# Attention in a fused two-layer block: scores from one 128-row product per head padded with zero rows, and row maxima from 48 rows in one half of the partitions, issued in twos behind two scores

## The reference, cut to what matters

```python
q = (x @ wq.T).reshape(B, S, 16, 8)          # B=4, S=1024, head size 8
k = repeat((x @ wk.T).reshape(B, S, 4, 8), 4) # four heads share one key/value head
v = repeat((x @ wv.T).reshape(B, S, 4, 8), 4)
attn = einsum('bqhd,bkhd->bhqk', q, k) / sqrt(8)
attn = softmax(where(causal, attn, -inf))
out = einsum('bhqk,bkhd->bqhd', attn, v).reshape(B, S, 128) @ wo.T
```

## Time and profile before

| | us |
|---|---|
| median of 3 runs | 1437.51 |
| lowest and highest | 1436.49, 1439.12 |
| profiled execution, span | 1437.3 |
| PE busy | 1150.2 (80%) |
| DVE busy | 1108.8 (77%) |
| ACT busy | 740.2 (51%) |
| POOL busy | 677.0 (47%) |

### The profile page before, as it was taken

The page is one execution under the profiler, slowest core; times in us unless marked ns, Lnnn a source line. Parts: engine busy times, 40 slices in busy tenths (PEclk is TensorE's granted clock), DMA queues, the critical chain, the costliest instruction groups (busy, mean ns, idle before and its releaser), DMA issues. The chain is left out here.

```text
span 1437.3 us, 18717 instructions
## 1 busy us (share of the span) xinstructions
PE 1150.2 (80%) x5568; PEld 535.7 (37%) x5568; DVE 1108.8 (77%) x3046; ACT 740.2 (51%) x1619; POOL 677.0 (47%) x823
## 2 busy tenths in 40 slices
PE   3613896899998997775747677998999899989885
PEld 1201454555554554331412322343334333433232
DVE  5889555655788879689897697788998889888227
ACT  4644676137435444342321157575567556755772
POOL 7524584364777778657670022215331533153312
PEclk9855997999999998787877589999999999999998
DMA  4000101422111110003123120303020302000002
GB/s 115 0 0 1 49 2 26 142 75 69 54 37 44 44 40 6 0 1 65 24 48 55 39 47 1 66 1 55 1 38 1 55 1 38 1 4 1 4 1 59
DMA packets 33682, 47.02 MB, mean 33 GB/s; under 512 B 5023, under 2 KB 18207, under 8 KB 33279
## 3 DMA queue, kind: packets, MB, share of 16 engines
q1 hardware_dynamic: 30990, 43.84, 13.8%
q10 hardware_dynamic: 2592, 2.00, 0.5%
HBM read 39.14 MB, written 6.68 MB: 32 GB/s over the span
## 5 line engine op out<-in xcount | busy, mean ns | idle before, releaser
L1694 ACT ACTIVATE RB<-PS 128x512 f32<-128x512 f32 (+3 forms) x768 | 323.2, 502 | 183.3 <-PE PS L676 180.4
L624 PE MATMUL PS<-B 96*128 96x512 bf16 (+3 forms) x768 | 247.6, 349 | 44.2 <-DVE SS L1191 14.7
L676 PE MATMUL PS<-B 96*128 96x512 bf16 (+3 forms) x768 | 238.3, 333 | 24.2 <-ACT RB L1694 22.2
L1191 DVE CUSTOM_DVE_ANT_0 PS<-PS,w_msk 128x128 f32<-128x128 f32 (+3 forms) x512 | 242.4, 505 | 18.6 <-PE PS L624 18.1
L1964 POOL TENSOR_SCALAR_AFFINE_SELECT RB<-RB 128x512 f32<-128x512 f32 x128 | 81.0, 635 | 363.9 <-ACT RB L1694 363.9
L1194 DVE TENSOR_REDUCE SS<-PS 128x1 f32<-128x512 f32 x256 | 175.6, 686 | 32.9 <-PE PS L624 31.9
L693 PE MATMUL PS<-RB,B 128*32 128x512 f32 (+3 forms) x1536 | 169.0, 514 | 0.0
L624 PEld LDWEIGHTS PS<-B 96*128 96x128 bf16 x768 | 75.0, 99 | 228.8 <-DVE SS L1191 99.7
L1870 POOL TENSOR_TENSOR RB<-RB,B 128x512 f32<-128x512 f32 x64 | 82.2, 1286 | 89.3 <-DVE RB L1020 66.8
L676 PEld LDWEIGHTS PS<-B 96*128 96x128 bf16 x768 | 73.6, 98 | 105.7 <-ACT RB L1694 74.6
L1536 ACT ACTIVATE RB<-PS 128x512 f32<-128x512 f32 x72 | 42.8, 595 | 129.6 <-PE PS L438 129.5
(11 more groups left out here) (262 smaller groups left out, 2209.9 us busy)
## 6 DMA issues: line engine op xcount, KB each, us to landing
B<-scrW SPq DMA_DIRECT2D x128, 128.0 KB, 3.0
B<-scrQ SPq DMA_DIRECT2D x72, 128.0 KB
scrQ<-B SPq DMA_DIRECT2D x6, 384.0 KB, 3.7
B<-scrK SPq DMA_DIRECT2D x36, 64.0 KB
X<-in_x SPq DMA_DIRECT2D x8, 256.0 KB, 8.7
out_dram<-X SPq DMA_DIRECT2D x7, 256.0 KB, 3.2
B<-in_w SPq DMA_DIRECT2D x3, 576.0 KB, 4.9
B<-in_zeros SPq DMA_DIRECT2D x9, 128.0 KB
```

Source lines behind the costliest of these rows:

```text
L624: pe.matmul(p[:, 0:w], qs[u % 3][:, h, 128 * i:128 * i + 128], keys_of(u, h)[:, 512 * c:512 * c + w], start=True, stop=True).then_inc(s["m ...
L676: pe.matmul(p[:, 0:w], keys_of(u, 4 * kl + z)[:, 128 * kt:128 * kt + 128], qs[u % 3][:, 4 * kl + z, 512 * qc + off:512 * qc + 512], start= ...
L1191: ins = dve.tensor_tensor_reduce(p, p, msk[:, 512 - w:512], 1.0, LOWEST, ALU.add, ALU.max, MX[:, u % 2, i, h, c:c + 1])
L1694: act.activation(RB[:, 4 * (step % 3) + z, 0:w], bank(bank_of["score", step, z])[:, 0:w], ACT.Exp).then_inc(s["ex2"], 1)
```

## The change

The rows of the contraction are laid out anew. `qs` and `kst` take all 128 partitions. For even heads (side 0) the nine product groups of 8 rows lie at rows 0 to 71, guard rows at 72 to 74, and zeros (ones in `kst`) down to 127. For odd heads (side 1) the first eight groups lie at rows 64 to 127, the ninth at 0 to 7, guard rows at 8 to 10, and zeros (ones) at 8 to 63. The six largest products come first, so they fill rows 0 to 47 for side 0 and 64 to 111 for side 1.

`score_2` contracts all 128 rows. `first_1` contracts only the 48 rows of the six largest products (the guard value that is subtracted from the scores leaves the three smallest out). Maxima are issued in twos, an odd head and an even head with the same tile, and on PE the order in a step becomes score, score, maximum, maximum, score, score, maximum, maximum. In steps 0 to 19 there are 4 or 6 maxima a step in place of 5.

So that heads of both key heads of a unit alternate, the columns of `wq` and the rows of `wo` are permuted on the host (`turn`). The `zrow` DMA falls away. `load_q` and `load_k` issue 18 DMAs of half the size; `fill_q` and `fill_k` issue 2 each, of 448 KB and 224 KB; the way home of the guard is 2 DMAs.

```diff
-        qs = [B[i][0:96, 0:4096].bitcast(BF).rearrange("p (h t) -> p h t", h=8) for i in (5, 1, 3)]
-        kst = [B[2][0:96, 2048 * i:2048 * i + 2048].bitcast(BF).rearrange("p (k t) -> p k t", k=4) for i in range(2)]
+        qs = [B[i][:, 0:4096].bitcast(BF).rearrange("p (s t) -> p s t", s=8) for i in (5, 1, 3)]
+        kst = [B[2][:, 2048 * i:2048 * i + 2048].bitcast(BF).rearrange("p (k l t) -> p k l t", k=2, l=2)
+               for i in range(2)]
...
-        FIRST = [(h, i, c) for h in range(8) for i in range(8) for c in range(i // 4 + 1)]
+        FIRST = [(2 * pair + side, i, c) for pair in range(4) for i in range(8) for c in range(i // 4 + 1)
+                 for side in (1, 0)]
+        PRODUCTS = [(0, 0), (0, 1), (1, 0), (1, 1), (0, 2), (2, 0), (1, 2), (2, 1), (2, 2)]
+        HIGHEST_ROWS = 48
+        GUARD_ROW = (72, 8)
+        SPARE_ROWS = (slice(72, 128), slice(8, 64))
+
+        def product_row(side, r):
+            return (64 * side + 8 * r) % 128
...
             if step < 20:
-                return [(1, n) for n in range(5 * step, min(5 * step + 5, 96))]
+                done = sum(6 if q % 5 in (1, 3) else 4 for q in range(step))
+                return [(1, n) for n in range(done, done + (6 if step % 5 in (1, 3) else 4))]
...
         def keys_of(u, h):
-            return kst[u // 2 % 2][:, 2 * (u % 2) + h // 4, :]
+            return kst[u // 2 % 2][:, u % 2, h % 2, :]
+
+        def queries_of(u, h):
+            return qs[u % 3][:, h, :]
+
+        def highest_rows(h):
+            return slice(64 * (h % 2), 64 * (h % 2) + HIGHEST_ROWS)
...
-                pe.matmul(p[:, 0:w], qs[u % 3][:, h, 128 * i:128 * i + 128],
-                          keys_of(u, h)[:, 512 * c:512 * c + w], start=True, stop=True).then_inc(s["mm1"], 1)
+                pe.matmul(p[:, 0:w], queries_of(u, h)[highest_rows(h), 128 * i:128 * i + 128],
+                          keys_of(u, h)[highest_rows(h), 512 * c:512 * c + w], start=True, stop=True).then_inc(s["mm1"], 1)
...
                 if u < 8 and r == 0:
-                    pe.wait_ge(s["gd1"], 16 * (u + 1))
-                for z in range(4):
-                    for v, n in ahead[z:z + 1]:
+                    pe.wait_ge(s["gd1"], 32 * (u + 1))
+                for half in range(2):
+                    for z in (2 * half, 2 * half + 1):
+                        if step < 192:
+                            score_2(step, z)
+                    for v, n in ahead[2 * half:2 * half + 2] if half == 0 else ahead[2:]:
                         first_1(next_1(step), v, n)
-                    if step < 192:
-                        score_2(step, z)
-                for v, n in ahead[4:]:
-                    first_1(next_1(step), v, n)
...
             def load_q(u):
                 b, hh = divmod(u, 2)
-                for a in range(3):
-                    for c in range(3):
-                        sp.dma_start(qs[u % 3][32 * a + 8 * c:32 * a + 8 * c + 8, :, :],
-                                     scrQ[b, a, 64 * hh:64 * hh + 64, :].rearrange("(h d) t -> d h t", d=8)).then_inc(
-                                         s_q[u % 3], 16)
-                if u >= 3:
-                    sp.dma_start(qs[u % 3][24:27, :, :], I["zrow"]).then_inc(s_q[u % 3], 16)
+                src = scrQ[b, :, 64 * hh:64 * hh + 64, :].rearrange("a (q l d) t -> a l d q t", q=4, l=2)
+                for r, (a, c) in enumerate(PRODUCTS):
+                    for side in range(2):
+                        o = product_row(side, r)
+                        sp.dma_start(qs[u % 3][o:o + 8, side:8:2, :], src[a, side, :, :, :]).then_inc(s_q[u % 3], 16)
...
-                sp.dma_start(qs[u % 3][24:27, :, :], scrM[u, :, :].rearrange("(a h) t -> a h t", h=8)).then_inc(s["gd1"], 16)
+                m3 = scrM[u, :, :].rearrange("(a q l) t -> l a q t", a=3, l=2)
+                for side in range(2):
+                    o = GUARD_ROW[side]
+                    sp.dma_start(qs[u % 3][o:o + 3, side:8:2, :], m3[side, :, :, :]).then_inc(s["gd1"], 16)
...
-    D["wqE"], D["wkE"], D["wvE"], D["woE"] = E("wq").T, E("wk").T, E("wv").T, E("wo").T
+    turn = np.arange(128).reshape(2, 2, 4, 8).transpose(0, 2, 1, 3).reshape(128)
+    D["wqE"], D["wkE"], D["wvE"], D["woE"] = E("wq").T[:, turn], E("wk").T, E("wv").T, E("wo").T[turn]
```

More of the change, by code:

```diff
@@ L629, in ready_1 @@
             def ready_1(u):
-                pe.wait_ge(s_q[u % 3], 192 + 160 * (u // 3))
-                pe.wait_ge(s_k[u // 2 % 2], 192 + 144 * (u // 4))
+                pe.wait_ge(s_q[u % 3], 32 + 288 * (u // 3 + 1))
+                pe.wait_ge(s_k[u // 2 % 2], 32 + 288 * (u // 4 + 1))
             value_c(0)
@@ L676, in score_2 @@
                 pe.matmul(p[:, 0:w], keys_of(u, 4 * kl + z)[:, 128 * kt:128 * kt + 128],
-                          qs[u % 3][:, 4 * kl + z, 512 * qc + off:512 * qc + 512],
+                          queries_of(u, 4 * kl + z)[:, 512 * qc + off:512 * qc + 512],
                           start=True, stop=True).then_inc(s["sc2"], 1)
@@ L692, in product_2 @@
                 for j in range(4):
-                    ins = pe.matmul(p[32 * j:32 * j + 32, off:off + w], VA[:, 8 * (u // 2) + kt, 2 * (u % 2) + kl, :],
+                    ins = pe.matmul(p[32 * j:32 * j + 32, off:off + w], VA[:, 8 * (u // 2) + kt, 2 * (u % 2) + j % 2, :],
                                     pb[:, j, 0:w], start=(kt == 0), stop=(kt == 4 * qc + 3), skip_group_check=True)
@@ L2008, in load_k @@
             def load_k(b):
-                for a in range(3):
-                    for c in range(3):
-                        sp.dma_start(kst[b % 2][32 * a + 8 * c:32 * a + 8 * c + 8, :, :],
-                                     scrK[c, :, 1024 * b:1024 * b + 1024].rearrange("(k d) t -> d k t", d=8)).then_inc(
-                                         s_k[b % 2], 16)
+                src = scrK[:, :, 1024 * b:1024 * b + 1024].rearrange("c (k l d) t -> c l d k t", k=2, l=2)
+                for r, (a, c) in enumerate(PRODUCTS):
+                    for side in range(2):
+                        o = product_row(side, r)
+                        sp.dma_start(kst[b % 2][o:o + 8, :, side, :], src[c, side, :, :, :]).then_inc(s_k[b % 2], 16)
             def load_q(u):
                 b, hh = divmod(u, 2)
-                for a in range(3):
-                    for c in range(3):
-                        sp.dma_start(qs[u % 3][32 * a + 8 * c:32 * a + 8 * c + 8, :, :],
-                                     scrQ[b, a, 64 * hh:64 * hh + 64, :].rearrange("(h d) t -> d h t", d=8)).then_inc(
-                                         s_q[u % 3], 16)
-                if u >= 3:
-                    sp.dma_start(qs[u % 3][24:27, :, :], I["zrow"]).then_inc(s_q[u % 3], 16)
+                src = scrQ[b, :, 64 * hh:64 * hh + 64, :].rearrange("a (q l d) t -> a l d q t", q=4, l=2)
+                for r, (a, c) in enumerate(PRODUCTS):
+                    for side in range(2):
+                        o = product_row(side, r)
+                        sp.dma_start(qs[u % 3][o:o + 8, side:8:2, :], src[a, side, :, :, :]).then_inc(s_q[u % 3], 16)
             def fill_q(u):
-                for a in range(3):
-                    sp.dma_start(qs[u][32 * a + 24:32 * a + 32, :, :], I["zeros"]).then_inc(s_q[u], 16)
+                for side in range(2):
+                    sp.dma_start(qs[u][SPARE_ROWS[side], side:8:2, :], I["zeros"]).then_inc(s_q[u], 16)
             def fill_k(b):
-                for a in range(3):
-                    sp.dma_start(kst[b][32 * a + 24:32 * a + 32, :, :], I["ones"]).then_inc(s_k[b], 16)
+                for side in range(2):
+                    sp.dma_start(kst[b][SPARE_ROWS[side], :, side, :], I["ones"]).then_inc(s_k[b], 16)
             def cuts_out(b):
@@ L2162, in arrays @@
     D["msk"] = np.concatenate([np.zeros((128, 384)), np.where(low, 0, -1e30)], axis=1).astype(bf)
-    D["zrow"] = np.zeros((3, 8, 1024), bf)
-    D["zeros"], D["ones"] = np.zeros((8, 8, 1024), bf), np.ones((8, 4, 1024), bf)
+    D["zeros"], D["ones"] = np.zeros((56, 4, 1024), bf), np.ones((56, 2, 1024), bf)
     return {k: np.ascontiguousarray(v) for k, v in D.items()}
```

## The result

The changed kernel takes **1483.4 us** (1479.7 to 1487.6) against 1437.2 for the kernel before on the same chip: a ratio of 1.0329, 95% interval 1.0301 to 1.0356, 46 us slower by the medians, 47 by the ratio. The prediction of 1442 us, with a range up to 1458, was wrong.

A forecast was written before the change was run, and what follows sets the result against it. PE and DVE were taken to pace the main stage in turn, PE's time counting in 63 of 164 steps. 1437.3 + 5 (rows, switches, overlap) + 0.3 (guard) = 1442.6, rounded down to 1442 us; range 1422 to 1458.

The forecast's parts named there:

- What bounds the kernel: Main stage, 820 to 1334 us: PE and DVE pace the loop in turn; ACT isn't the pace.
- the 63 waits of DVE: Main stage: DVE waits for a maximum's matmul, 45.2 us in all; PE time counts only in 63 of 164 steps.
- Overlap: A step's two pairs on PE: matmuls in opposite halves run side by side, saving 0.32 us a step.
- The stagger of the second start: Second matmul of a pair on PE: starts 0 to 0.05 us later; 0.03 us a step taken.
- Switches: PE's changes of array layout in a step: two round trips of 0.245 us less one 0.12 us switch, +0.37 us.
- The rival of cheap switches: Going to halves by rows costs as little as maximum to score: 1419 us, or 1430 at half price; chance 0.30.
- that of halves that don't overlap: Each maximum keeps its 0.163 us and layout changes come on top: 1461 us; chance 0.09.
- Net of the rows: PE in the main stage: -0.32 + 0.37 + 0.03 = +0.08 us a step, counted in 63 steps, +5 us.
- The order: PE's step, score, score, pair, score, score, pair, product: priced by added layout changes only, +0.37 us a step.
- the rival of a DVE that starves at the head of a step: First maximum behind two scores and a layout change, 0.53 us later: 33 us at worst, 1470; chance 0.07.
- Loads, guard, the stretch before 820: Twice the DMAs on SP and 740 to 820 us: nothing; the guard's way home, exposed once: +0.3 us.
- What I had said would show it wrong: Score to pair at most 0.22 us, pair's starts a full matmul apart, or DVE's waits moving over 15 us.

The follow-up runs named there:

- seven switches: The kernel before with its maxima's matmuls contracting rows 0 to 47 in place of 0 to 95, order as before: 1584.4 us, ratio 1.1068.
- the pair first: The changed kernel with PE's order maximum, maximum, score, score, twice in a step: 1454.8 us, ratio 1.0115; the same list and order on 96 rows: 1453.5 us.
- the fifth bank: Exponentials over 32 columns, five banks for maxima, two for scores: the kernel before, 1415.8 us; the same with order score, score, maximum, maximum, 1426.8 us.

## Why the prediction was wrong, point by point

- **What bounds the kernel: half right.** PE and DVE pace the loop in turn, and the stage's length is DVE's work plus DVE's idle time. But counting the 63 waits of DVE as the only steps in which PE's time counts was too mild. Of 54 us of PE time by the overlap, 27 showed up in the total; of 115 us by seven switches, all did, and more. The text also took the two of a pair to run one by one wherever PE waits for a bank; the starts lie over 0.1 us apart in only 25 of 336 pairs, so the overlap came nearly everywhere.
- **Overlap: right.** 0.33 us a step was taken, and the pair occupies the time of one matmul. The stagger of the second start is 3 or 4 ns in 302 of 336 pairs, less than the 0.03 us a step that I took.
- **Switches: right in kind and nearly in size.** 0.37 us more a step was taken from the value product's rows. Measured are 0.10 and 0.11 us for in and out of the half array, and 0.10 from a pair of 256 columns to the value product (1105.77 to 1105.98). Four of these, less the 0.095 from score to value product that falls away, make 0.32 us. By the Trainium skill (TensorEngine Tiling (Array Packing), Key Properties) a change of mode drains TensorE, with no figure; the trace agrees in that each change to or from 64-row tiles costs time, with these numbers. The rival of cheap switches falls, and so does that of halves that don't overlap. The Trainium skill has about 4 ns between the starts of tiles in separate row groups (TensorE: Matmul & The Clock Gate, Part 3); the trace agrees, with 3 or 4 ns.
- **Net of the rows: +5 us taken, 10 to 14 measured** in the order of the change, about 0 with the pair first. The term counted PE's time in 63 steps, whatever the order. Its PE time was too high, too: with the measured switches (0.32 us) against the overlap (0.33) PE's balance is about nothing, so the 10 to 14 us aren't PE's columns and switches by their sum. What they are stays open; the granted clock is 0.93 with the rows and 0.95 with list and order alone.
- **The order: this is the step that failed.** The sum priced it at nothing beyond its switches, since the maxima's number and widths stay the same and DVE has four banks. It was kept as the rival of a DVE that starves at the head of a step, with 33 us at worst and a chance of 0.07. Measured by itself it is 27 us, at 96 rows and without any switch. The rival's reason was only partly right, too: the maximum's place behind one score costs 4 us at most. It costs when scores and maxima go in twos: then, as I read it, DVE's supply comes in lumps, with value product, small products and two scores between. The sign that was in the trace before: DVE already waited 63 times, so its four banks ran empty about every third step, and a cushion that is empty so often can't take a longer pause. That this is the whole mechanism isn't shown: the fifth bank took off about 10 of 20 us, within wide noise.
- **The list: 6 us, not priced at all.** The text took the maxima's order as free.
- **Loads, guard, the stretch before 820: right.** 0.4 us against 0.3; 740 to 820 has DVE at 62.98 against 62.35 us, and the main stage starts 0.4 us later (821.11 against 820.73).
- **What I had said would show it wrong did.** DVE's waits moved by 43 us, where 15 was the bound.

In sum: 27 (order) and 6 (list) make 33 us, and 34 were measured for both together. The rows' 10 to 14 us are what is left of the 46, not a measurement of their own.

**Left open.** What the other half of the order's price is once ACT and the fifth bank are taken out. Why two scores ahead of two maxima cost some 16 us more than two maxima ahead of two scores (1.0234 against 1.0126, list included), although the cycle has the same longest run: in the first, the small products of `post_h` and `heads_2` stand right behind the pair and ask for banks of the same ring. PE's waits for DVE at such small products are 26.3 us in the first and 21.3 in the second, which is 5 of the 16, and no run took them away. The clock's own part wasn't separated from the idle time that goes with it: 78 us at 1.2 GHz in place of 31, at half the columns, can be up to some 23 us of PE's time, an estimate. No variant was faster than the kernel before with its work intact.

## What to carry to other kernels

When two engines pass work through a small ring of banks, price the order of issue like an instruction: lay out the longest stretch in which the producer makes nothing for the consumer, and compare it with the ring. That stretch doesn't tell all: two orders with the same longest one lay 16 us apart here. Waits of the consumer in the profile, however short each, say that the ring already runs empty. A saving by tiles side by side has to pay for its changes of layout: here two pairs (0.33 us saved) against three more changes (0.32 us) was no gain. Longer runs of one layout save changes, but the one run that tried it (four maxima, four scores) lost 42 us more, with longer waits for ACT's and DVE's banks.

## What the runs showed of the hardware

A change between a matmul over half of the array's rows and one over all of them cost TensorE 0.10 to 0.11 us beyond the columns, each way, at a granted clock of 1.00. At 0.50 it was 0.11 us: the kernel with 48-row maxima in the old order has 0.54 us from a 512-column maximum to the score behind it (1002.45 to 1002.99), of which 512 columns at 1.2 GHz are 0.43.

Two 48-row matmuls in opposite halves occupied the time of one, with starts 3 or 4 ns apart in 302 of 336 pairs. From the start of two in the same half to the next score it was 0.53 us, where from the pair it is 0.33.

A PE that is busy by the profile can be at 1.2 GHz. In the kernel with seven more switches a step the granted clock was 0.50 for 102.7 us on end, with PE busy in all of them. It had not stood idle just before: from 945 to 959 us it was busy 14.00 of 14 us, at a clock of 0.63, and from 925 to 945 us 18.05 of 20, at 1.00. The granted clock of the main stage went from 0.97 to 0.95 with the order alone, 0.93 in the changed kernel and 0.85 with the seven switches. Whether the clock falls because of the changes of layout or of the short waits, no run shows.
